# Graph attention in windows: edge lengths multiplied into the turned weights instead of the gathered rows

## The reference

```python
edge_features = concatenate([h[dst], h[src] * dir_w, dir_w, lower_adj_feat], axis=-1)
edge_attr = edge_features @ W_ee + b_ee
for i in range(3):
    q, k, v = ...                              # of the layer's input h_cur
    e = edge_attr @ We[i] + be[i]
    alpha = (q[dst] * (k[src] + e)).sum(-1) / sqrt(128)
    w = softmax of alpha over the edges of one dst
    out = segment_sum((v[src] + e) * w, dst)   # mean over the heads
    h_cur = relu(out + h_cur @ Ws[i] + bs[i] + residual)
```

## Time and profile before

| | |
|---|---|
| time, median of 3 | 4367.01 us (4362.61 to 4374.62) |
| the profiled execution | 4329.4 us, of which its span (first to last instruction) 4327.6 us |
| PE busy | 3495.6 us, 81% of the span |
| DVE busy | 1823.4 us, 42% |
| ACT busy | 1433.0 us, 33% |
| POOL busy | 1862.8 us, 43% |
| granted TensorE clock, mean | 0.916 of 2.4 GHz |

### The profile page before, as it was taken

The page is one execution under the profiler, slowest core; times in us unless marked ns, Lnnn a source line. Parts: engine busy times, 40 slices in busy tenths (PEclk is TensorE's granted clock), DMA queues, the critical chain, the costliest instruction groups (busy, mean ns, idle before and its releaser), DMA issues. The chain is left out here.

```text
span 4327.6 us, 82914 instructions
## 1 busy us (share of the span) xinstructions
PE 3495.6 (81%) x22381; PEld 2067.5 (48%) x22381; DVE 1823.4 (42%) x5369; ACT 1433.0 (33%) x3483; POOL 1862.8 (43%) x1907
## 2 busy tenths in 40 slices
PE   4999999947758888876777777667777769999998
PEld 2666666635534444443444444334443444555564
DVE  4666666647523333332333333323333323344222
ACT  3555555522623333332233323222222223122112
POOL 2555555500256665653566656456666630000000
PEclk8999999979879999998888998878898889999999
DMA  5677775656444554555666666556666645443223
GB/s 139 187 200 199 198 196 167 165 115 204 140 136 137 140 136 131 139 137 136 169 176 172 176 175 179 156 155 167 167 164 168 166 111 176 171 177 118 74 97 125
DMA packets 716528, 675.29 MB, mean 156 GB/s; under 512 B 382359, under 2 KB 542945, under 8 KB 716117
## 3 DMA queue, kind: packets, MB, share of 16 engines
q1 hardware_dynamic: 622598, 466.26, 37.1%
q0 software_dynamic: 77008, 200.24, 17.2%
q10 hardware_dynamic: 16768, 6.91, 0.6%
HBM read 530.84 MB, written 142.28 MB: 156 GB/s over the span
## 5 line engine op out<-in xcount | busy, mean ns | idle before, releaser
L2293 POOL DMA_INDIRECT l_y<-s_lrows,l_src x1344 | 1352.6, 1006 | 964.3 <-issue 352.4
L2373 PE MATMUL ps<-l_y,aw_pT 128*63 128x277 f32 x2700 | 436.8, 467 | 259.9 <-ACT aw_pT L2591 249.1
L3404 PE MATMUL ps<-nl_adj,nl_table 126*128 126x504 bf16 (+1 forms) x3150 | 631.4, 357 | 2.3 <-DVE nl_table L3639 2.3
L998 POOL DMA_INDIRECT em_gs<-s_rows,em_idx x400 | 432.3, 1081 | 325.8 <-DVE em_a L1189 147.9
L2357 PE MATMUL ps<-aw_yT,aw_qt 128*63 128x384 f32 x1800 | 377.2, 529 | 120.0 <-DMA aw_yT<-s_dxT 61.2
L3404 PEld LDWEIGHTS ps<-nl_adj,nl_table 126*128 126x128 bf16 x3150 | 301.8, 96 | 299.0 <-issue 5.3
L2750 DVE COPY aw_axd<-ps 128x252 f32<-128x252 f32 x225 | 94.7, 421 | 796.9 <-remote 409.9
L2330 PE MATMUL ps<-ident,l_y 128*128 128x128 f32 x1800 | 281.5, 292 | 150.9 <-issue 83.1
L2373 PEld LDWEIGHTS ps<-l_y,aw_pT 128*63 128x63 f32 x2700 | 195.7, 154 | 431.9 <-ACT aw_pT L2591 279.6
L2591 ACT ACTIVATE aw_pT<-ps 128x381 f32<-128x381 f32 x225 | 109.9, 488 | 736.8 <-remote 506.0
L2577 ACT ACTIVATE aw_yT<-ps 128x512 f32<-128x512 f32 (+1 forms) x525 | 261.4, 536 | 245.2 <-remote 114.7
(11 more groups left out here) (381 smaller groups left out, 5866.1 us busy)
## 6 DMA issues: line engine op xcount, KB each, us to landing
nl_adj<-s_adj SPq DMA_DIRECT2D x20, 3100.8 KB
aw_yT<-s_dxT SPq DMA_DIRECT2D x150, 384.0 KB
aw_geoS<-s_geoS SPq DMA_DIRECT2D x450, 94.5 KB
nl_adj<-s_adj SPq DMA_DIRECT2D x15, 2325.6 KB
ws_msg<-s_msg SPq DMA_DIRECT2D x75, 384.0 KB, 3.8
s_dxT<-aw_yT SPq DMA_DIRECT2D x75, 384.0 KB
aw_qt<-s_qt SPq DMA_DIRECT2D x225, 126.0 KB
s_msg<-em_msg SPq DMA_DIRECT2D x100, 256.0 KB
```

The lines of the kernel that those rows point to most:

```text
L998: pool.indirect_dma_start(out=gs[:, u, j, :], out_offset=None, in_=d["rows0"], in_offset=bass.IndirectOffsetOnAxis(ap=slot[:, u, 2 * j:2 * ...
L2293: pool.indirect_dma_start(out=y[:, u, j, 0:W], out_offset=None, in_=table, in_offset=bass.IndirectOffsetOnAxis(ap=src[:, u, j:j + 1], axis ...
L2373: m = nc.tensor.matmul(k.ps[64 * v:64 * v + HW, SUM, 0:SW], pT[:, SLOT[u], j, 64 * v:64 * v + HW], y[:, u, v * TH + j, 0:SW], start=j == 0 ...
L3404: m = nc.tensor.matmul(k.ps[:, bank(i, p), 0:cols * WN], source[:, p, q, b, :], adj[:, a % 2, 0:cols, b * WN:(b + 1) * WN], start=b == 0 a ...
```

## The change

In layers two and three the multiplication of the gathered initial rows (`weigh`, DVE) is gone. After ACT has copied the turned weights of a window to `pT`, DVE reads the same PSUM bank, multiplies by the edge lengths (`weigh_weights`) and writes a second set of weights `pE`. The message sums become twelve products: six with `pT` over 149 columns (edge numbers and current row), six with `pE` over 128 columns (the initial row, now unscaled). To make the first six contiguous, `y` is laid out anew: edge numbers in columns 3 to 23, rows from column 24 (`ROW`). This layout holds in layer one too. The turned weights stand 128 columns apart in PSUM instead of 127. The semaphores of the query mixing are merged into `mixed` and `mixed_c`.

```diff
+ROW = GK + 3
-    G0 = 2 * D
+    G0 = ROW - GK
+    pE = sb("pE", [128, 3, TH, V, 64])
-    ready = steps("ready", ["DX", "SEL", "OFF"], U, NW)
+    ready = steps("ready", ["DX", "SEL", "OFF"] if l == 0 else ["SEL", "OFF"], U, NW)
+    if l:
+        pE_ok = steps("pE_ok", ["P"], U, NW)
...
-                pool.indirect_dma_start(out=y[:, u, j, 0:W], out_offset=None, in_=table,
+                pool.indirect_dma_start(out=y[:, u, j, ROW:ROW + W], out_offset=None, in_=table,
...
         def turn_weights(w, u):
             pe.wait_ge(exped.sem, exped.of(w, "E"))
             pe.wait_ge(pT_ok.sem, pT_ok.of(w - 1, "P"))
+            if l:
+                pe.wait_ge(pE_ok.sem, pE_ok.of(w - 1, "P"))
             for j in range(TH):
-                m = nc.tensor.transpose(k.ps[:, TURN, j * M:(j + 1) * M], p[:, SLOT[u], j * 128:(j + 1) * 128], k.ident[0:M, 0:M])
+                m = nc.tensor.transpose(k.ps[:, TURN, j * 128:j * 128 + M], p[:, SLOT[u], j * 128:(j + 1) * 128], k.ident[0:M, 0:M])
...
         def sums(w, u):
...
             for j in range(TH):
                 for v in range(V):
-                    m = nc.tensor.matmul(k.ps[64 * v:64 * v + HW, SUM, 0:SW], pT[:, SLOT[u], j, 64 * v:64 * v + HW],
-                                         y[:, u, v * TH + j, 0:SW], start=j == 0, stop=j == TH - 1)
+                    m = nc.tensor.matmul(k.ps[64 * v:64 * v + HW, SUM, 0:SW if l == 0 else GK + D], pT[:, SLOT[u], j, 64 * v:64 * v + HW],
+                                         y[:, u, v * TH + j, G0:G0 + (SW if l == 0 else GK + D)], start=j == 0, stop=l == 0 and j == TH - 1)
+            if l:
+                pe.wait_ge(pE_ok.sem, pE_ok.of(w, "P"))
+                for j in range(TH):
+                    for v in range(V):
+                        m = nc.tensor.matmul(k.ps[64 * v:64 * v + HW, SUM, GK + D:SW], pE[:, SLOT[u], j, v, 0:HW],
+                                             y[:, u, v * TH + j, ROW + D:ROW + 2 * D], start=False, stop=j == TH - 1)
             m.then_inc(summed.sem, 1)
...
         def mask(w, u):
             s = ready.sem
+            if l and started(w, U):
+                dve.wait_ge(summed.sem, summed.of(w - U, "AG"))
...
+        def weigh_weights(w, u):
+            dve.wait_ge(pT_ok.sem, pT_ok.of(w, "P"))
+            dve.wait_ge(summed.sem, summed.of(w - 2, "AG"))
+            nc.vector.tensor_tensor(pE[:, SLOT[u], :, :, 0:HW],
+                                    k.ps[:, TURN, 0:TH * 128].rearrange("p (j v m) -> p j v m", v=V, m=64)[:, :, :, 0:HW],
+                                    bc(y[:, u, :, G0:G0 + 1].rearrange("p (v j) o -> p j v o", v=V), [128, TH, V, HW]),
+                                    ALU.mult).then_inc(pE_ok.sem, 1)
...
             if not (isinstance(w, int) and w == NW - 1):
-                weigh(w + 1, (u + 1) % U, i if u < U - 1 else i + 1)
+                if l == 0:
+                    weigh(w + 1, (u + 1) % U, i if u < U - 1 else i + 1)
                 mask(w + 1, (u + 1) % U)
             if started(w, 1):
                 denominator(w - 1, (u - 1) % U)
             maximum(w, u)
+            if l and started(w, 1):
+                weigh_weights(w - 1, (u - 1) % U)
```

More of the change, by code:

```diff
@@ L2330, in turn_features @@
                     m = nc.tensor.transpose(k.ps[:, FEATURES[n], q * 128:(q + 1) * 128],
-                                            y[:, u, j, what * D:(what + 1) * D], k.ident[:, :])
+                                            y[:, u, j, ROW + what * D:ROW + (what + 1) * D], k.ident[:, :])
                 m.then_inc(turned.sem, 1)
@@ L2390, in turn_sums @@
                 pe.wait_ge(parts_ok.sem, parts_ok.of(w - 2, "AG"))
-            for n, (at, rows) in enumerate(((0, D), (D, D), (2 * D, GK))):
+            for n, (at, rows) in enumerate(((GK, D), (GK + D, D), (0, GK))):
                 m = nc.tensor.transpose(k.ps[0:rows, TS[u], 128 * n:128 * n + M], agr[:, SLOT[u], at:at + rows], k.ident[0:M, 0:M])
@@ L2513, in turn @@
                 if queries:
-                    pe.wait_ge(query_mixed_c, 7)
+                    pe.wait_ge(mixed_c, steps + 7)
                 pe.wait_ge(mixed_c, steps)
@@ L2829, in vector @@
             before.scalar_done(dve)
-        for s in (ready, soft, indexed, parts_ok, out_ok) + ((geo_ok,) if queries else (joined_ok,)):
+        for s in (ready, soft, indexed, parts_ok, out_ok) + ((pE_ok,) if l else ()) + ((geo_ok,) if queries else (joined_ok,)):
             s.prime(dve)
@@ L2839, in vector @@
             dve.sem_inc(indexed.sem, U)
-        weigh(0, 0, 0)
+        if l == 0:
+            weigh(0, 0, 0)
         mask(0, 0)
@@ L2843, in vector @@
         c = NWC - 1
+        if l:
+            weigh_weights(NW - 1, U - 1)
         denominator(NW - 1, U - 1)
```

32 lines of the change are left out of this document (16 added, 16 removed).

## The result

The changed kernel takes 4398.87 us (median of 5 runs, 4391.82 to 4409.63) where the kernel before, run beside it, takes 4372.28 us (5 runs). The ratio is 1.0059, 95% interval 1.0037 to 1.0081: slower by 0.6%. The forecast was 4351 us and faster. The profiled execution took 4396.09 us, with a span of 4394.3 us.

What follows compares the result with a forecast made beforehand. A chain of waits, in many windows paced by POOL (7.5 us of gathers plus about 2 us until release), was taken as the bound. Terms -31 + 12 + 3 = -16 us took 4367 to 4351 us, range 4310 to 4383.

Steps and rivals of the forecast that it cites:

- The holds go: Layers two and three: without the old multiplication, gathers lose 23 and 18 us of 48 us of holds.
- The new multiplication: VectorE, layers two and three: 378 elements from PSUM take 0.56 us, bounds 0.42 and 0.94.
- Twelve products: PE's message sums: 0.05 us more in 66 windows not paced by POOL, 3 us, bounds 0 and 13.
- Sums that wait for VectorE: About 13 layer-two turns after a geometry split: PE 1.8 us late each, 12 us counted, bounds 0 and 23.
- The rival built on it: Message sums wait for VectorE in 28 layer-two turns, costing 35 us against 15 us gained: 4387 us, chance 0.17.
- In windows paced by POOL all of it: Layers two and three: shorter gathers count fully in POOL-paced windows, half in others: 16 and 15 us, sum 31 us.
- round and release follow one another: POOL-paced windows: PE's signals come only after the gather round, 7.5 us of gathers plus about 2 us.
- Nothing moves: Layers two and three: ended holds only become longer waits for PE's signals; 4367 us or up to 8 more, chance 0.21.
- The check that I had named: Layer three: last gather to next maximum stays 2.4 us; if it grows by what gathers lost, nothing moves.

Runs made afterwards that it cites:

- pair of dummies: Two kernels without the edge-length multiplication in layers two and three, plus an unused VectorE instruction with two SBUF inputs (0.9982 of before) or one (1.0035).
- free group: Group of runs in which PE's signals aren't late; the kernel before took 3761 and 3763 us there.
- held group: Group of runs in which PE's signals are late; the kernel before took 4324 to 4335 us in four such groups.
- second test: Held group: changed kernel again 1.0053, with indices copied early 1.0089, without edge-length multiplication 1.0047, with second weights unused 1.0051, all against before.
- e8_pE_unused_2: Changed kernel with second weights made and waited for, but six products with `pT` alone: 1.0051 of the kernel before, held group.
- one-input dummy: Kernel without edge-length multiplication in layers two and three, plus an unused VectorE reduction with one SBUF input: 1.0035 of the kernel before, held group.
- no multiplication: New layout, six products, no edge-length multiplication in layers two and three: 0.9868 of the kernel before in a free group, 1.0047 in a held group.
- half rows: Kernel without edge-length multiplication in layers two and three, its gathers there bringing half the bytes, from wrong rows: 1.0056 of the kernel before, held group.
- two-input dummy: Kernel without edge-length multiplication in layers two and three, plus an unused VectorE multiplication with two SBUF inputs: 0.9982 of the kernel before, held group.
- fill kernels: Changed kernel with GpSimd fills, held groups, against before: before the sixth gather 1.0057; before every gather 0.9934 (384 elements) or 1.0041 (256).
- e2_split: Kernel before with the new layout and twelve products, all with `pT`, rows multiplied as before: 1.0002 of the kernel before, free group.

## Why the prediction was wrong, step by step

**The holds go: right.** The mean gather fell from 1.01 and 1.00 to 0.949 us over both layers, 47.7 us less in all where 48 had been read. The rule of the Trainium skill on instructions with two SBUF inputs ("SBUF — State Buffer", "Who interferes with whom") holds here, and the pair of dummies shows it by itself: 1009 ns with two inputs, 952 with one.

**The new multiplication: right.** 0.552 us, forecast 0.56.

**Twelve products: right, and nothing.** 1.63 us for both groups, forecast at most 1.82. The 62 ns a pass that the Trainium skill gives with hardware decode off ("TensorE: Matmul & The Clock Gate", "Wait — 56ns, not 53.3ns?") don't bind here: the second six products, of two passes each, start 109 ns apart, 55 ns a pass, and the total didn't grow. (Whether decode was off in these runs isn't on record.) The kernel with twelve products alone has 1.0002 in a free group; in the held group of the second test the changed kernel and the one with six products, otherwise alike (e8_pE_unused_2), took 4360.53 and 4356.51 us, and their intervals overlap.

**Sums that wait for VectorE: too dear.** Forecast 13 turns of 1.8 us, 12 us of them in the end. PE waited for `pE` 26 times, 16.3 us in all, over both layers, and with and without the product the kernels are within 0.2% of each other in a free group (0.9850, 0.9868) and in a held one (1.0051, 1.0047). The rival built on it, slower at 4387 us, came nearest to the time but by the wrong mechanism.

**The step that failed** is "In windows paced by POOL all of it": round and release follow one another, so the 41 us of shorter gathers put to this line (of 48) give 31 us. I had read "2.4 us after the last gather" as fixed. That was a misreading of the earlier trace rows to begin with: the maximum starts 2.42 us after the last gather in one round and 2.75 us (3013.51 - 3010.76) in the other. And both rounds are 6.26 us long (the first began at 3004.50), so they can't tell a distance from the last gather from one from the first. The experiments told them apart. In a held group a round of six gathers is answered about 8.7 to 9.0 us after its first gather, though holds, a fill or six fills make the round up to 1 us longer. 81.6 us of fills cost nothing. So the 48 us were not on the path: that is the rival "Nothing moves", whose condition was just this, signals with a time of their own. The check that I had named, the distance from the last gather to the next signal in layer three, went from 2.42 to 2.64 us in the rounds shown, and the medians over both layers from 2.23 to 2.66: by what the rounds lost (0.18) and 0.2 us more.

**What neither forecast nor rival had** is that the holds were worth something. Without them the kernel is 0.35 to 0.55% slower (one-input dummy, no multiplication, half rows), with useless ones it is as before. The trace shows one way in which a held gather can help: it is a gap in the row of gathers of the same kind as a spacing above 1.5 us. In the two-input dummy kernel, GpSimd, PE and ACT:

```profile
2601.55 0.95 POOL L2296 DMA_INDIRECT l_y<-s_lrows,l_src  x1 [0.30 <-issue]
2602.80 1.99 POOL L2296 DMA_INDIRECT l_y<-s_lrows,l_src  x1 [0.30 <-issue]
2605.09 0.94 POOL L2296 DMA_INDIRECT l_y<-s_lrows,l_src  x1 [0.30 <-issue]
...
2601.94 0.82 PE L2333 MATMUL ps<-ident,l_y 128*128 128x128 f32 x6
...
2603.96 0.87 ACT L2580 ACTIVATE aw_yT<-ps 128x512 f32<-128x512 f32 x2 [1.00 <-PE ps L2333]
```

PE's transposes end at 2602.76, and the signal reaches ACT at 2603.96, in the middle of the held gather, and not after the round; GpSimd goes on without a pause. Most of the difference lies in layer two, where VectorE's geometry work makes such encounters long: there GpSimd waited for another engine 77 times in 440 gathers before and 75 in 450 with the useless instruction, but 84 in 426 with the one-input dummy and 92 in 434 with the change, that is 1.05 and 1.00 times against 1.18 and 1.27 a window. In layer three it is 1.03 and 1.04 against 1.02 and 1.14: there the one-input dummy shows no difference. That this accounts for all of the 0.5% is argued from these counts, not shown: a spacing in the fill kernels changes other things too, and a hold can't be placed at will.

**Left open.** What it is that works the gathers off at 1.45 us each, and why one group of runs has it and another not, on the same chip, no run shows. It isn't the moving of the rows: in the trace of before the first DMA packet of a gather is recorded 1.91, 1.73, 1.69, 1.75, 1.73 and 1.66 us after its start for the first to the sixth of a burst (medians), so the transfers don't pile up. Also open is why PE itself pauses in the changed kernel: 57.9 + 51.0 + 47.8 us "issue" before its transposes, masks and scores from 2041 to 3480 us, against 28.2 + 6.4 + 4.3 us without the multiplication, in timelines like the one above with instructions 1.4 us apart (3119.30, 3120.65, 3122.04). The kernel with six products that waits for `pE` (e8_pE_unused_2) has 25.6 + 7.7 + 2.7 us there, and the twelve products in a free group (e2_split) have no such pauses, so they come with twelve products where signals are late. They cost little: that kernel took 1.0051 where the change took 1.0053. The changed kernel by itself was never measured in a free group; from its parts (0.9850 with the product, 1.0002 with twelve products) I estimate 0.985 there.

## What to carry to other kernels

A fixed distance in a trace has two ends: before a gain is counted on it, look for two rounds of unequal length and see which distance stays. Idle time that follows a burst of work can belong to the burst's beginning, and then a shorter burst gives nothing, and a somewhat longer one, or a spaced one, costs nothing (81.6 us of fills here). And a saving on an engine that runs ahead and then waits for an answer is worth what the answer's time allows: test it with a fill of known length before building the real change.

## What the runs showed of the hardware

- The same kernel, before, took 3761 and 3763 us in two groups of runs and 4324 to 4372 us in the others, 13 to 14% less time (3763 / 4324 = 0.870, 3761 / 4372 = 0.860). Two of the chips were in a group of either kind at different times. So a ratio of such a kernel holds for its own group alone: the same edit gave 0.9868 and 1.0047, another 1.0575 and 0.9934.
- In the slower groups signals from PE to the other engines came late while GpSimd issued gathers 1.25 us apart (3.7 us from 3108.68 to 3112.42 above; median 1.60 us over the two layers in the trace of before), and in the others within 0.03 us (2706.38 to 2706.41) beside the same gathers.
- A burst of gathers was answered about 1.45 us per gather after its first (medians 5.4 to 6.0 us for four, 8.7 to 9.0 for six), however long the burst took (6.25 to 7.22 us for six), and with 64 KB a gather as with 128.
- Fills of GpSimd between gathers, 393 us in all, made the changed kernel 1.6% faster than without them in a held group.
